# A recommendation model's forward pass: a table load on another queue, fewer zero multiplies, nine crossed tiles instead of ten, and a last layer summed by TensorE

## The reference

```python
wide = dense @ Wd_wide
for si, wi in zip(S, w):
    wide = wide + wi[si]
wide = wide + wc0[S[3] * VOCABS[4] + S[4]]
wide = wide + wc1[S[5] * VOCABS[6] + S[6]]
deep_in = jnp.concatenate([dense @ Wd_deep] + [Ei[si] for Ei, si in zip(E, S)], axis=1)
h = jax.nn.relu(deep_in @ W1)
h = jax.nn.relu(h @ W2)
deep = h @ W3
return bias + deep + wide
```

## Time and profile before

| | us |
|---|---|
| median of 3 runs | 123.77 |
| lowest, highest | 123.75, 123.79 |
| the profiled execution | 123.86 |
| its span | 122.1 |
| TensorE busy | 118.2 (97% of the span) |
| VectorE busy | 86.8 (71%) |
| ScalarE busy | 57.9 (47%) |
| POOL busy | 98.0 (80%) |

### The profile page before, as it was taken

One profiled execution on the slowest core, in us unless ns is written; L12 is line 12 of the kernel. 1 busy time (PEld: TensorE's weight loads), 2 busy tenths in 40 slices (PEclk: granted clock), 3 DMA queues, 4 the chain that ended last, 5 costly groups with the idle time before them and its releaser, 6 DMA issues.

```text
span 122.1 us, 1847 instructions
## 1 busy us (share of the span) xinstructions
PE 118.2 (97%) x615; PEld 92.4 (76%) x615; DVE 86.8 (71%) x205; ACT 57.9 (47%) x105; POOL 98.0 (80%) x138
## 2 busy tenths in 40 slices
PE   6999999999999999999999999999999999999991
PEld 2665865877878886888888785888888886888881
DVE  3299998958999976949998335949997026529342
ACT  1599998179574424058090153058090150307130
POOL 6688778888898888988998888988888888888000
PEclk9999999999999999999999999999999999999999
DMA  3979765479423242213233322200000000000000
GB/s 72 364 121 272 177 136 89 80 193 408 84 22 22 21 71 27 23 12 23 22 27 71 22 22 23 19 4 0 3 6 0 0 0 0 0 0 6 0 0 3
DMA packets 5833, 7.47 MB, mean 61 GB/s; under 512 B 2636, under 2 KB 3532, under 8 KB 5824
## 3 DMA queue, kind: packets, MB, share of 16 engines
q0 software_dynamic: 2240, 1.61, 16.0%
q1 hardware_dynamic: 3152, 5.02, 12.5%
q10 hardware_dynamic: 432, 0.72, 1.9%
HBM read 7.32 MB, written 0.03 MB: 60 GB/s over the span
## 4 chain that ended last, share of the span: by engine, by line
PE 97%; DVE 1%; ACT 0%; issue 0%
PE l_ps L864 18%; PE l_ps L866 18%; PE l_ps L865 17%; PE io_ps L810 15%; PE io_ps L858 8%; PE io_ps L822 4%; PE io_ps L961 3%; PE l_ps L918 3%; PE io_ps L833 2%; PE io_ps L943 1%; PE l_ps L795 1%; PE l_ps L876 1%; PE l_ps L978 1%; PE l_ps L877 1%; PE l_ps L883 1%; PE io_ps L954 1%
## 5 line engine op out<-in xcount | busy, mean ns | idle before, releaser
L548 DVE TENSOR_SCALAR onehot<-idx_bc,row_id 128x512 fp32r<-128x512 f16 x76 | 38.2, 566 | 2.2 <-PE io_ps L822 2.1
L364 POOL DMA_INDIRECT x_pair<-in_rows_dram,idx_gather x32 | 32.5, 1016 | 6.5 <-issue 6.5
L355 POOL MEMSET pause_sb<- 128x320 f32 (+1 forms) x57 | 25.5, 448 | 0.0
L375 POOL DMA_INDIRECT cross<-in_wc_dram,idx_cross x22 | 21.1, 958 | 3.6 <-issue 3.6
L864 PE MATMUL l_ps<-xt_hi,w_hi 128*128 128x512 f32 x60 | 23.9, 398 | 0.0
L866 PE MATMUL l_ps<-xt_hi,w_lo 128*128 128x512 f32 x60 | 23.6, 394 | 0.0
L865 PE MATMUL l_ps<-xt_lo,w_hi 128*128 128x512 f32 x60 | 23.5, 392 | 0.0
L810 PE MATMUL io_ps<-onehot,table_hl 128*128 128x512 f32 x76 | 21.5, 408 | 0.0
L364 POOL DMA_INDIRECT x_two<-in_rows_dram,idx_gather x16 | 16.9, 1058 | 4.1 <-issue 2.9
L406 ACT CAST xt_hi<-io_ps 64x512 fp32r<-64x512 f32 x20 | 11.6, 579 | 15.7 <-PE io_ps L810 15.6
L810 PEld LDWEIGHTS io_ps<-onehot,table_hl 128*128 128x128 f32 x76 | 14.2, 188 | 4.5 <-DVE onehot L548 1.6
(11 more groups left out here) (98 smaller groups left out, 148.6 us busy)
## 6 DMA issues: line engine op xcount, KB each, us to landing
idx_bc<-idx_dram SPq DMA_DIRECT2D x3, 640.0 KB, 6.5
dense_x<-in_dense_x_dram SPq DMA_DIRECT2D x4, 154.0 KB
table<-in_wc_rows_dram SPq DMA_DIRECT2D x1, 564.0 KB, 4.7
w_sb<-in_w_dram ACTq DMA_DIRECT2D x2, 256.0 KB, 5.1
w_sb<-in_w_dram SPq DMA_DIRECT2D x2, 256.0 KB, 4.2
x_pair<-in_rows_dram,idx_gather POOLq DMA_INDIRECT x32, 3.3
w_sb<-in_w_dram SPq DMA_DIRECT2D x1, 512.0 KB, 4.7
table<-in_small_dram SPq DMA_DIRECT2D x1, 416.0 KB, 4.3
```

The costliest lines, as they stand in the source:

```text
L355: nc.gpsimd.memset(pause_sb[:, 0:columns], 0.0).then_inc(paused, 1)
L364: nc.gpsimd.indirect_dma_start(out=x_two[:, t // 2, t % 2 * ROW:(t % 2 + 1) * ROW] if f == 2 else x_pair[:, t, f * ROW:(f + 1) * ROW], out ...
L375: nc.gpsimd.indirect_dma_start(out=cross[:, c, t:t + 1], out_offset=None, in_=wc[c], in_offset=bass.IndirectOffsetOnAxis(ap=idx_cross[:, c ...
L548: nc.vector.tensor_scalar(onehot[:, CHUNK0[i] + c, :], idx_bc[:, b % (BLOCKS - 1), i, :], row_id[:, c:c + 1], None, ALU.is_equal).then_inc ...
```

## The change

Five edits. Table 0 is loaded by SP right behind the indices, ahead of the rest of the tables; ScalarE makes a one-column copy in its place, ahead of the loads of W1. TensorE's first zero multiplies are five instead of eight. Nine tiles are crossed in SBUF instead of ten, so POOL gathers one value column more, and the place (3, 3) is empty. The pauses behind block 3's row gathers have 224 columns instead of 320. In the last block VectorE weighs h2's second half for the first 256 samples only; for the other 256 TensorE adds h2 times W3's column to the sum by ones (layer3_sum and layer3_weigh in place of layer3).

```diff
-WARM_UP = 8
+WARM_UP = 5
...
-XTILES = 10
+XTILES = 9
...
-ONEHOT_BLOCKS = (1, 2)
+ONEHOT_BLOCKS = (1, 2, 3)
...
-           (3, 0): [6], (3, 1): [7], (3, 2): [8], (3, 3): [9]}
+           (3, 0): [6], (3, 1): [7], (3, 2): [8]}
...
             sp.dma_start(idx_raw[:], index).then_inc(index_loaded, 16)
+            sp.dma_start(table[:, 0:CA], small[:, 0:CA]).then_inc(table_loaded[0], 16)
             sp.dma_start(table[:, CA:], small[:, CA:]).then_inc(table_loaded[1], 16)
...
             act.wait_ge(warm_up_ready, 1)
-            act.dma_start(table[:, 0:CA], small[:, 0:CA]).then_inc(table_loaded[0], 16)
+            nc.scalar.copy(first_copy[:], zero16[:, 0:1])
...
             def weigh_second(b):
                 dve.wait_ge(h2_used, b * M2 + 1)
-                for part in parts(b, 1):
+                for part in (None, ) if b + 1 < BLOCKS else (0,):
...
-            dve.wait_ge(last_done, len(pieces))
+            dve.wait_ge(last_done, 1)
...
-            def layer3(b, part):
+            def layer3_sum(b, part, first):
+
                 use = ("last", b, 0)
-                pe.wait_ge(h2_used, (b + 1) * M2 + part)
-                if part == 0:
+                pe.wait_ge(h2_used, b * M2 + 1 + (part == 0))
+                if first:
                     pe.wait_ge(ones_ready, 1)
                     io_free(use)
-                for at in range(samples(part).start, samples(part).stop, P):
+                s = samples(part)
+                for at in range(s.start, s.stop, P):
+
                     last = nc.tensor.matmul(io_bank(use)[:, at // P:at // P + 1], wide_deep_look[b % 2][:, at:at + P],
-                                            ones[:], start=True, stop=True)
+                                            ones[:], start=first and at == s.start, stop=False)
+
+            def layer3_weigh(b, part):
+
+                use = ("last", b, 0)
+                pe.wait_ge(h2_ready, b * M2 + 2 + part)
+                s = samples(part)
+                for at in range(s.start, s.stop, P):
+                    last = nc.tensor.matmul(io_bank(use)[:, at // P:at // P + 1], h2[:, 1, at:at + P], w3_sb[:, 1:2],
+                                            start=False, stop=at + P == s.stop)
                 last.then_inc(last_done, 1)
...
-            for part in parts(BLOCKS - 1, 1):
-                layer3(BLOCKS - 1, part)
+            layer3_sum(BLOCKS - 1, 0, True)
+            layer3_sum(BLOCKS - 1, 1, False)
+            layer3_weigh(BLOCKS - 1, 1)
```

More of the change, by code:

```diff
@@ L191, in program @@
         ones = sb("ones", [P, 1], f32)
+        first_copy = sb("first_copy", [P, 1], f32)
         pause_sb = sb("pause_sb", [P, PAUSE], f32)
```

## The result

Over 20 executions each on one chip, the kernel before took 123.80 us in the median (from 123.57) and the changed one 122.89 us (from 122.05). The ratio is 0.9898, with a 95% interval of 0.9875 to 0.9921: 1.26 us less (the interval is 0.98 to 1.55). The two medians by themselves are 0.91 apart. Ratios here leave out executions in which the chip ran disturbed (over 1.5% above the quickest); the medians do not. The forecast was 121.3 us, 2.5 us less. The sign is right and the size is half. The ratio times 123.77 is 122.5, inside the range; the plain median of 122.89 lies 0.2 us above its upper end.

A forecast was written before the change was run, and what follows sets the result against it. It took TensorE's own work, 97% of the chain, as the bound. From 123.86 us it took 1.04 + 0.06 + 0.38 + 1.0 = 2.48, and 0.09 for the median: 121.3 us, range 120.6 to 122.7.

The forecast's parts named there:

- Tenth crossed tile: Last block, between layers 1 and 2: six TensorE multiplies go, 1.04 us back, plus 0.06 for the tile's row spread.
- POOL: One more gather, 1.49 us, and shorter block 3 pauses, about 1.0 back: costs nothing, with two microseconds of cover.
- The end: Last sums: VectorE's second-half weighing goes, TensorE's eight passes hold it until about 119.0; 0.38 us gained, bounds 0.2 to 0.54.
- The head: Start of the kernel until block 0's pairs are turned: 1.0 us gained, bounds 1.5 and -0.3.
- Step (b): ScalarE in the head: W1's loads issued at about 2.3, ScalarE 0.3 to 0.9 earlier, with VectorE's lead 0.7 to 1.3.
- Step (a): Table 0 on SP's queue: lands in 2.5 us, at 3.7 instead of 5.3, so VectorE starts 1.5 us earlier.
- W1's load or table 0 binds the head anyway: Rival, chance 0.13: W1's load is later and the table's 4.1 us may not shrink; head 0.2, total 122.1.
- Step (c): Gathered rows of block 0: TensorE's turn of the pairs can come about 1.03 us earlier, plus slack behind it.
- (d): TensorE's clock in the head: with five zeros and a 0.3 us gap, risen by 6.9 as before, it holds nobody up.
- the late-clock rival: Rival, chance 0.22: the clock rises near 10 in the head, multiplies run at half speed; head -0.3, total 122.6.
- the third rival: Rival, chance 0.03: clock held low much longer, kernel slower from a rise after 13.3; 124.8 with one at 15.

The follow-up runs named there:

- W1 held: Changed kernel with W1's two loads on ScalarE's queue held until the first copy has run: 121.92 us, ratio 0.9836; 0.9840 on the third chip.
- head undone: Changed kernel with eight zeros, table 0 back on ScalarE's queue and no first copy: 122.26 us, ratio 0.9854; 0.9900 on the third chip.
- W1 held and reordered: W1 held, plus ScalarE's group-2 cast and VectorE's low part of W1 put later: ratio 0.9823 on the second chip, 0.9856 on the third.
- the six profiles: Profiles of the changed kernel and five follow-ups with both nine tiles and the new end: 97.68 to 97.74 us from the turn of block 0's pairs on.

## Why the prediction was half right

**Tenth crossed tile, 1.04 and 0.06: right.** Layer 2 begins with no wait, nothing took the tile's place, and the tile alone measured 1.1 us.

**POOL: right in what counts.** The last gather starts at 113.02, not 112.5, and lands at about 115.3, by the 2.3 us of its kind. VectorE takes it at 116.50 without a wait, with 1.2 us of cover left instead of the two that the prediction names. The pauses of block 3 were never run alone, so what they contribute is open.

**The end, 0.38: right**, 1.77 to 1.39. Eight passes hold TensorE until ScalarE's half is there, as worked out.

**The head, 1.0: wrong**, and this is the whole error: 2.48 less 1.0 is 1.48, inside the interval of the measured 1.26. Three steps of it failed. The range held the result only because it took in the rivals; its own range for the forecast (120.6 to 121.9) did not.

*Step (b)*, "and only then issues W1's groups 2 and 3, at about 2.3 instead of 1.59". They went out at 1.18, earlier than before. The prediction took the order of the instructions on ScalarE's stream for the order in time. The row shows that an issue with no wait of its own is not held by computing instructions ahead of it. The Trainium skill (Advanced Engine Details and Errata, "Sequencer and Instruction Queues") says as much: the sequencer pushes an engine instruction into a queue and reads on. The issue at 1.18 inside a table load of 0.74 to 2.02 agrees. Before, the table load stood behind the issues, so the earlier trace rows could not show it. The size of this step was too high as well. With the loads issued at 2.25, as it assumed, ScalarE's cast of group 2 came at 6.57, 0.27 earlier than before, which is the low end of its 0.3 to 0.9. VectorE could not run ahead by the further 0.44, for it waited 0.71 us, until 10.97, for an index copy of ScalarE's. TensorE began layer 1 at 9.77 instead of the kernel before's 10.35, 0.58 earlier, where the step has 0.7 to 1.3.

*Step (a)*, "it is second on that queue with nothing beside it". Being alone on SP's queue is not being alone. With W1's loads on their way at the same time table 0 took 3.9 us (3.8 to 4.1 when it was on ScalarE's queue), and ahead of them 2.5, as forecast (3.3 on the third chip). The Trainium skill (DMA: Bandwidth & Descriptors, "Issuing engines are not separate DMA queues") says that transfers from all issuers interleave on the same DMA engines. 3.9 against 2.5 agrees. So the rival "W1's load or table 0 binds the head anyway", with its chance of 0.13, is what came true for the table, and by its own price of 0.2 it would have put the kernel at 122.1.

*Step (c)*, "POOL's gathers of block 0 are not moved, so this turn can come earlier by about 1.03". This is no fixed room. Their rows were 0.39 later in the changed kernel's profile, and 0.23 later in the one that holds W1. And the prediction names one meeting with the rows where there are two. The last of the four gathers for the first turn took 5.4 us from issue to landing before, and was there 0.9 ahead of TensorE's 14.39. Issued at the same 8.09 it took 6.0 with W1 held, and TensorE waited for it; with the head undone it took 3.6. A slack that is read in one execution is no constant where the work that makes it varies so much. Whether holding W1 made that landing later, no run shows.

**The clock, (d): right.** Five zeros and eight gave the same, 122.28 and 122.26 us on one chip. The rise shows in the spacing, not in the granted clock, which is 1.0 throughout: in the changed kernel the two busy zeros at 5.31 take 0.59 together, where the first ones, at the lower level, begin 0.43 apart (1.59, 2.02). The look-ups came 0.94 us after TensorE was free, held by one-hots and not by the clock. When the clock rises differs from one execution to the next whatever the zeros: eight of them took 3.59 us before and 3.28 with the head undone, so in the latter it rose within them, and with W1 held and reordered (five zeros) the two at 5.78 still took 1.06. The rule of the Trainium skill (TensorE: Matmul & The Clock Gate, "What's actually happening") that speaks against fewer zeros would have given 1.2 in all, near the measured 1.26, and the late-clock rival 122.6, near the 122.5 of the ratio, but both for a wrong reason: eight zeros did not bring the head's microsecond back. One sum of the third rival is off: if 2.7 us more use up the gain behind a rise at 10, the kernel is slower from a rise at 12.7 on, not 13.3. Nothing else rests on it.

**What stays open.** Against a 1.5 that the six profiles show behind the turn, the ratio gives 1.26, with 1.5 inside its interval. The changed kernel's executions that the ratio counts scatter from 122.05 to 123.48, while the six of the head undone on the first chip lay within 0.33 us. The tables' second part landing at 7.3, just when ScalarE wants it (7.32), and with the eight zeros later than wanted, may be a source of that scatter, and the gathers another. Both were seen in profiled executions only, and neither is shown for the others. With one of W1's loads issued later the scatter stayed.

## What to carry to other kernels

An issue of a transfer that has no wait does not stay behind the computing instructions written ahead of it (1.18 against 2.03 us here); to delay it, put a semaphore between. Before pricing an earlier load, list what is in flight on all queues at that moment, not on its own, and before pricing an earlier engine, find out what the second-latest arrival is at each meeting point behind it, the nearest first, and how far its own durations vary over several executions. And an execution's time less the start of a late meeting point (here 97.7 for six profiles) can tell within a few hundredths which half of a change worked, where medians argue about half a microsecond. It is no constant of the kernel either: on other chips it came out up to 1.2 higher.

## What the runs showed of the hardware

- ScalarE's queue issued two loads at 1.18 us while ScalarE loaded its function table (0.74 to 2.02); with a semaphore on the copy behind it they went out at 2.25.
- A load of 192 KB took 3.8 to 4.1 us with W1's 512 KB issued within half a microsecond of it, and 2.5 to 3.3 us when those were issued 1.06 us later. Which of the two queues it was on made no difference (3.8 to 4.1 on ScalarE's, 3.9 to 4.1 on SP's).
- The price was paid by the next load as well: 416 KB took 5.6 to 6.1 us behind table 0 on SP's queue, 4.0 to 4.3 with the table on the other, 3.6 behind it again with W1 held.
- One POOL gather of the same size took between 0.94 and 3.27 us beside VectorE's stream; two stretched ones moved the issue of block 0's last by a microsecond (19.51 to 20.53), and the landing of its rows by 0.39.
- The fourth gather of block 0 took 3.6 to 6.0 us from issue to landing (head undone 3.6, before 5.4, W1 held 6.0).
